# The routing of the first five batches in the attention stage, its parts laid on other steps

## What is computed

```
x = x + 0.5 * ffn(layernorm(x))
x = x + attn(layernorm(x))
x = x + 0.5 * ffn(layernorm(x))
```

```
top1 = argmax(softmax(xt @ w_router));  gate = probs[top1]
pos  = cumsum(onehot(top1), axis=0)[token, top1] - 1
slot = top1 * C + pos   if pos < C
```

## Time and profile before

| what | value |
|---|---|
| median of three runs | 1595.82 us (1594.23 to 1596.99) |
| the profiled execution | 1598.67 us, its span 1596.9 us |
| TensorE's mean granted clock | 0.894 of full speed |
| busy shares of the span | PE 84%, DVE 79%, ACT 73%, POOL 48% |
| attention stage, about | 690 to 1192 us of the span |

### The profile page before, as it was taken

One profiled execution on the slowest core, in us unless ns is written; L12 is line 12 of the kernel. 1 busy time (PEld: TensorE's weight loads), 2 busy tenths in 40 slices (PEclk: granted clock), 3 DMA queues, 4 the chain that ended last, 5 costly groups with the idle time before them and its releaser, 6 DMA issues. The chain is left out here.

```text
span 1596.9 us, 31540 instructions
## 1 busy us (share of the span) xinstructions
PE 1335.5 (84%) x10174; PEld 1245.1 (78%) x10174; DVE 1265.6 (79%) x3493; ACT 1167.6 (73%) x2486; POOL 769.8 (48%) x917
## 2 busy tenths in 40 slices
PE   4536623999999999499999999996729999999997
PEld 3324313999999999489989888986619999999997
DVE  6576852999999999458899999999847778777775
ACT  6849933777777777379998898885647777777774
POOL 0057773344434444314447777776552433443443
PEclk8555555999999999799999999998859999999999
DMA  9999754667667667331222332211134443544551
GB/s 362 395 303 324 242 186 137 223 192 247 221 193 243 220 201 248 102 96 41 80 75 86 97 95 84 77 52 58 32 114 125 131 141 112 149 142 118 145 150 30
DMA packets 196882, 250.41 MB, mean 157 GB/s; under 512 B 24650, under 2 KB 182008, under 8 KB 192624
## 3 DMA queue, kind: packets, MB, share of 16 engines
q1 hardware_dynamic: 169072, 204.49, 41.1%
q0 software_dynamic: 27648, 43.91, 8.3%
HBM read 128.18 MB, written 152.47 MB: 176 GB/s over the span
## 5 line engine op out<-in xcount | busy, mean ns | idle before, releaser
L1035 PE MATMUL ps<-xs,ws 128*128 128x320 f32 x3072 | 464.7, 310 | 0.3 <-issue 0.2
L1035 PEld LDWEIGHTS ps<-xs,ws 128*128 128x128 f32 x3072 | 454.7, 189 | 1.2 <-issue 1.2
L368 POOL DMA_INDIRECT slots<-xn,r x256 | 262.6, 1026 | 199.7 <-issue 76.4
L850 POOL DMA_INDIRECT x_rows<-ys,oidx x160 | 165.3, 1033 | 242.6 <-DVE ys L973 203.1
L850 POOL DMA_INDIRECT out<-ys,oidx x160 | 155.9, 974 | 246.8 <-DVE ys L962 184.3
L1035 PE MATMUL ps<-ws,hs 128*128 128x256 f32 x1920 | 262.1, 288 | 10.4 <-DVE ys L962 1.7
L1035 PEld LDWEIGHTS ps<-ws,hs 128*128 128x128 f32 x1920 | 239.2, 190 | 23.7 <-issue 22.1
L871 ACT CAST xs<-ps 128x512 fp32r<-128x512 f32 (+1 forms) x192 | 98.5, 514 | 129.9 <-PE ps L1028 129.9
L985 DVE TENSOR_TENSOR hf<-ps,sg 128x320 f32<-128x320 f32 x256 | 125.4, 490 | 85.2 <-ACT sg L904 84.5
L436 PE MATMUL ps<-cf,xn 128*128 128x128 f32 x512 | 111.2, 357 | 85.8 <-ACT xn L390 85.8
L925 DVE TENSOR_TENSOR ws<-wraw,ws 128x512 fp32r<-128x512 f32 x192 | 132.6, 692 | 58.2 <-ACT ws L864 55.5
(11 more groups left out here) (135 smaller groups left out, 2494.2 us busy)
## 6 DMA issues: line engine op xcount, KB each, us to landing
slots<-zero SPq DMA_DIRECT2D x32, 1300.0 KB, 19.0
xg<-slots SPq DMA_DIRECT2D x62, 650.0 KB
x_rows<-x SPq DMA_DIRECT2D x32, 516.0 KB, 10.7
x<-x_rows SPq DMA_DIRECT2D x32, 516.0 KB, 4.9
x<-in_x SPq DMA_DIRECT2D x32, 512.0 KB, 11.3
wraw<-in_w_gate SPq DMA_DIRECT2D x64, 256.0 KB, 2.8
wraw<-in_w_up SPq DMA_DIRECT2D x64, 256.0 KB, 3.3
wraw<-in_w_down SPq DMA_DIRECT2D x64, 256.0 KB, 3.3
```

Source lines behind the costliest of these rows:

```text
L368: nc.gpsimd.indirect_dma_start(out=self.slots, out_offset=bass.IndirectOffsetOnAxis(ap=self.slot[:, t % self.xr, k:k + 1], axis=0), in_=se ...
L850: nc.gpsimd.indirect_dma_start(out=rows, out_offset=bass.IndirectOffsetOnAxis(ap=OIDX[:, e % YR, k:k + 1], axis=0), in_=YS[:, e % YR, k, : ...
L1035: ins = pe.matmul(dst, left(a, k), right(b, k), start=(n == 0), stop=(n == len(terms) - 1))
```

## The change

The parts of the five wide choices get other steps, part 1 is split in two, the count stands two steps later, and the scatters one. The new part 7 is the second half of part 1 (L508, L510, L513). Modulo 8 the wide choices stand after the change: part 0 in step 7, part 1 (L505 alone) and part 3 in 0, part 7 in 3, part 2 in 4, part 4 and the count in 5, parts 5 and 6 in 6, the scatters in 7, 0, 1, 2, 3, 4, 5. The other choices and the first stage issue part 7 directly after part 1, as before. The loop's own work, the instructions and their number stay.

```diff
@@ post: the second half of part 1 is part 7
                     dve.scalar_tensor_tensor(cand, d, 0.0, mid(REV, n), ALU.is_ge,
                                              ALU.mult).then_inc(self.chosen.sem, 1)
+                if step == 7:
                     dve.wait_ge(self.chosen.sem, self.chosen.at(c + 1))
                     dve.reduce_max(rr, cand, AX).then_inc(links.sem, 1)
@@ route
-                                for part in ((0,), (1, 2), (3, 4), (5, 6))[q]:
+                                for part in ((0,), (1, 7, 2), (3, 4), (5, 6))[q]:
@@ attention
-                POST_AT = [(15, 16, 17, 19, 20, 20, 21) if wide else (15, 16, 16, 17, 17, 19, 19) if t < BATCH - 2
-                           else (15, 16, 16, 17, 17, 17, 17) for wide, (t, lo, hi) in zip(SPREAD, CHOICES)]
-                COUNT_AT = [19 if t < BATCH - 2 else 17 for t, lo, hi in CHOICES]
+                POST_AT = [(15, 16, 20, 16, 21, 22, 22, 19) if wide else (15, 16, 16, 17, 17, 19, 19, 16) if t < BATCH - 2
+                           else (15, 16, 16, 17, 17, 17, 17, 16) for wide, (t, lo, hi) in zip(SPREAD, CHOICES)]
+                COUNT_AT = [21 if wide else 19 if t < BATCH - 2 else 17 for wide, (t, lo, hi) in zip(SPREAD, CHOICES)]
 
                 def pairs_at(u):
-                    return [22 + max(0, u - 1) if wide else n + 1 + u for wide, n in zip(SPREAD, COUNT_AT)]
+                    return [23 + max(0, u - 1) if wide else n + 1 + u for wide, n in zip(SPREAD, COUNT_AT)]
@@ attention, vector: the order at the end of a step
-                        for part in (3, 4, 5, 6, 1, 2, 0):
+                        for part in (3, 4, 5, 6, 1, 7, 2, 0):
                             chosen(S, part, False)
-                        for part in (4, 6, 1, 2, 3, 0):
+                        for part in (4, 6, 1, 7, 2, 3, 0):
                             chosen(S, part, True)
```

## The result

The changed kernel takes 1601.15 us (median of 7 runs, 1598.83 to 1603.61) against 1595.82 us before. The ratio is 1.0038, with a 95% interval of 1.0028 to 1.0047 (it isn't the quotient of the two medians, which is 1.0033). The changed kernel is slower by 0.4% where no measurable change was forecast, and its median lies 1 us above the top of the range. The profiled execution took 1603.61 us, with a span of 1601.8.

The account below looks back on a forecast made before the run. DVE was taken to bound the attention stage step by step. Moved work 0, split -0.5 and hits -0.6 sum to -1.1 us, giving 1594.7 us against the median 1595.82; range 1591.3 to 1600.2 us.

Parts of the forecast that it names:

- DVE is the bound, and moving its work within a period changes nothing: Attention stage: each step lasts as long as DVE's work in it, so the moved work costs 0 us.
- The forecast of the steps: Eight attention steps after the change: 6.82, 5.84, 8.05, 7.09, 7.08, 6.43, 8.47, 6.67 us, sum 56.45 against 56.56.
- The split, -0.5 us: L505 apart from its dependent follower L508 saves DVE 0.10 us a batch, 0.5 us over five.
- PE and ACT at nothing: Shortest steps 7, 0, 1: PE falls 0.6 us behind, catches up in step 2; uncovered, 3 us.
- I take half of the gain, 0.6 us: DVE's `mix` in step 4 no longer lengthened by POOL's scaling: -0.6 us, bounds 1.2 gained and 1.2 lost.
- more hits: Slower rival: four `mix` a period lengthened by POOL instead of one, 0.30 us each, +4.0 us, 1599.8 us, chance 0.07.
- Its point of decision: The slower rival decides from the fourth `mix` hit in a period; from the third at 0.5 us each.
- the rule of the Trainium skill: DVE instruction with two SBUF inputs contends with GpSimd reading SBUF; the later waits for the whole other, some 0.5 us.
- The ring: Step 6: ACT's norm waits 0.6 us for the last scatter pair, covered; as slower rival 1599.7 or 1604.7 us, chance 0.13.
- POOL's own count: POOL's work from `pool_rstd` in step 7 to the base's end in step 4: 39.7 us becomes 42.3.

Follow-up runs that it names:

- split_only: Kernel before with only DVE's parts rearranged (part 3 in step 0, part 7 in step 1), slot numbers, count and scatters kept: 1596.00 us, ratio 1.0004.
- the three edits: Kernel before with, separately, base scaling ahead of the scatters (1593.58 us), `a_rstd` moved into step 6 (1596.41 us), scatters one step later (1603.15 us).
- all fourteen traces: One profiled execution each of the kernel before, the changed kernel and every follow-up kernel; steps 15 to 54 took 282.26 to 294.92 us.

## Why the prediction was wrong, point by point

**DVE is the bound, and moving its work within a period changes nothing: right.** The forecast of the steps held to 0.1 us in all but one once the scaling was out, and the parts alone with POOL's steps kept gave 1.0004.

**The split, -0.5 us, and PE and ACT at nothing: not contradicted.** `split_only` shows no gain, but 0.5 us is below what it can tell. No wait for PE appeared in the stretch.

**"I take half of the gain, 0.6 us", bounded "by as many again (1.2 us lost)": this is the step that failed.** The term came out at +7.3 us of excess in place of -0.6, six times its upper bound. Two errors are in it. I counted hits from `mix` alone, at 0.30 each, because that was the one which repeated in the trace of before. In the changed kernel the scan, `a_factors` and part 2 are held as well, the longest of them by 0.39 to 0.47 us an instruction. With the scatters alone moved it is part 6, by 0.29 to 0.42, and L505 of part 1, by 0.20 to 0.24, too. And I took the few hits of before as a typical number. But 2.6 us of hits in 284 is a favourable position: each of the three edits that shifted POOL's work in the kernel before raised it, to 3.3, 4.6 and 10.9 us. As far as three edits tell, a shift was more likely to find a worse position than a better one, and I had given both the same weight.

**The rival "more hits" had the mechanism, with a chance of 0.07 that was too low**, and a price (+4.0 us, 1599.8) that was low by 1.3 us against the measured median. Its point of decision, the fourth `mix` hit in a period, was wrong: two hit `mix` and four or five others sufficed. What speaks for the rule of the Trainium skill that I set beside it (SBUF — State Buffer, Who interferes with whom) is now more than two instructions getting longer: L536 above ends within 0.01 us of the end of the scatter that it met. The trace agrees with the page that the later one waits for the end of the other. In these rows the price goes by the rest of the other's time, so a small operation can pay more than a large one. The rule as I had put it, two SBUF inputs, is too narrow for these runs: L536 and L542 (TENSOR_SCALAR) and L544 (CAST) have one input, and took 0.45 to 0.52 us in place of 0.14 to 0.17.

**The ring.** I forecast a wait of 0.6 us at ACT, covered by 1.8 us. ACT waited 10.4 us in four cases, up to 2.9, and `mix` 0.4 us more than usual in three of five periods: 1.2 us in all. In one of the three the kernel before waits as long, 0.53 us, so against it the ring costs some 0.8 us. The mechanism was right and "cost at nothing" nearly so; the wait was mis-sized since POOL took longer than worked out: 42.3 us in my sum, and 46.1 from 950.34 to the end of the scaling at 996.4. The landings were not slow: where the trace has them, the scatter waited for landed 2.1 us after its start, against a median of 2.3.

**POOL's own count** erred for the same reason: its instructions get longer as well where they meet DVE's, so its lateness grows with what it causes.

## What to carry to other kernels

When a change shifts one of VectorE and GpSimd against the other, list the instructions of both in the stretch and treat the number of meetings as open: bound it by what all the eligible instructions could cost (the last section tells which those were here), not by what the present alignment happens to cost. An alignment with few meetings is worth keeping, and the cheap thing to vary is the order within GpSimd's steps, which changes neither work nor dependencies and moved the time of the changed kernel by 0.4%, from a ratio of 1.0038 to 0.9997. Where GpSimd serves two consumers from one queue (here the factors of the norm and the scatters), anything that makes it wait holds the other too.

## What the hardware showed that I had not expected

Which of VectorE's instructions were held divides sharply. Over steps 15 to 54 of all fourteen traces, `softplus`, `x_lo` and `x_new`, which take one of their inputs from PSUM, ran 2,240 times, 1,966 of them beside an instruction of POOL, and none took over 0.03 us more than usual; neither did the statistics (L245), in 1,120. The scan and `mix`, with both inputs in SBUF, also ran 2,240 times, and 172 took over 0.045 us more, up to 0.56.

Operations of VectorE on 2 to 16 elements per partition, 0.16 us alone, took 0.45 to 0.62 us beside POOL's work. The scaling of x, 1.1 us a step on an engine that isn't the bound, is worth 4 us of the kernel's time before the change and 10 us after it (1601.15 to 1591.22).

It is mutual and includes the scatters. VectorE ran the bf16 scan of part 2 in the changed kernel:

```profile
992.81 1.26 DVE L517 TENSOR_TENSOR_SCAN r<-fresh,r 128x544 bf16<-128x544 bf16 x1
```

POOL's scatter beside it is the one at 992.80 above. It started at nearly the same time and took 2.07 us in place of 0.97, while the scan kept its usual length.
